# Denominators of a softmax from a running sum over four key tiles in place of two pair sums, with the tasks of a software pipeline moved to other slots

## The reference

```python
xt = jnp.transpose(x, (0, 2, 1))                 # 512 tokens, 256 channels
q = xt @ Wq.T
qh = q.reshape(B, T, 8, 32).transpose(0, 2, 1, 3)
scores = scale * jnp.einsum('bhqd,bhkd->bhqk', qh, qh)
logits = (scores * cmask + (1.0 - cmask) * NEG) * rmask
attn = jax.nn.softmax(logits, axis=-1)
ctx = jnp.einsum('bhqk,bhkd->bhqd', attn, qh)
out = ctx.reshape(...) @ Wo.T                    # and x = x + out, transposed back
```

## Time and profile before

| | |
|---|---|
| median of 3 runs | 2805.89 us (2802.98 to 2807.58) |
| profiled execution | 2816.45 us, its span 2814.6 us |
| TensorE matmul busy | 2633.3 us, 94% |
| VectorE busy | 2097.5 us, 75% |
| ScalarE busy | 1348.0 us, 48% |
| GpSimd busy | 914.2 us, 32% |
| mean granted TensorE clock | 0.984 |
| denominators' products (L706) | 480 passes, 605 ns each |
| adds on GpSimd (L407) | 120, 2349 ns each |

### The profile page before, as it was taken

How to read it: one execution, slowest core, us unless ns; L and a number is a source line. 1 busy time by engine, 2 the same in 40 slices (tenths; PEclk the granted TensorE clock), 3 DMA queues, 4 the chain that set the end, 5 groups by cost and what they waited for, 6 DMA issues and landing times. The chain is left out here.

```text
span 2814.6 us, 108219 instructions
## 1 busy us (share of the span) xinstructions
PE 2633.3 (94%) x46966; PEld 1503.7 (53%) x46966; DVE 2097.5 (75%) x4263; ACT 1348.0 (48%) x2344; POOL 914.2 (32%) x830
## 2 busy tenths in 40 slices
PE   8999999999989999999999999997999999999986
PEld 4333333333379898989999898983222222222221
DVE  5766666666788887888888887755777777777785
ACT  2555555555322222222322222211888787887876
POOL 1444444444022222222222222111244344344333
PEclk9999999999799999999999999998999999999999
DMA  2310111101100000000000000004344444544532
GB/s 66 94 55 28 54 37 46 55 28 43 27 14 0 0 0 0 0 0 0 0 0 0 0 0 0 0 5 108 74 107 116 107 106 112 114 104 112 115 91 52
DMA packets 120897, 132.05 MB, mean 47 GB/s; under 512 B 31800, under 2 KB 84944, under 8 KB 120674
## 3 DMA queue, kind: packets, MB, share of 16 engines
q1 hardware_dynamic: 114942, 123.12, 17.1%
q10 hardware_dynamic: 5760, 6.56, 0.8%
HBM read 85.29 MB, written 44.30 MB: 46 GB/s over the span
## 5 line engine op out<-in xcount | busy, mean ns | idle before, releaser
L912 PE MATMUL exp_ps<-region,gru_hT 128*16 128x128 f32 x16384 | 498.5, 274 | 39.3 <-DVE gru_hT L1039 7.8
L1582 DVE TENSOR_REDUCE x<-exp_ps 128x2 f32<-128x1024 f32 x352 | 426.0, 1221 | 104.8 <-PE exp_ps L1693 104.3
L912 PEld LDWEIGHTS exp_ps<-region,gru_hT 128*16 128x16 f32 x16384 | 428.3, 103 | 107.8 <-DVE gru_hT L1039 107.8
L845 POOL TENSOR_TENSOR xT<-xT,gru_hT 128x64 f32<-128x64 f32 x256 | 181.0, 707 | 824.6 <-DVE gru_hT L1039 815.6
L1508 ACT ACTIVATE region<-exp_ps,x 128x1024 f32<-128x1024 f32 x336 | 370.2, 1110 | 72.8 <-PE exp_ps L1664 72.8
L407 POOL TENSOR_TENSOR l_probs<-l_probs 128x1024 f32<-128x1024 f32 x120 | 281.1, 2349 | 297.7 <-ACT l_probs L483 220.1
L958 ACT ACTIVATE gru_r<-exp_ps 128x128 f32<-128x128 f32 x256 | 70.9, 277 | 588.1 <-PE exp_ps L912 588.1
L593 DVE TENSOR_REDUCE l_maxes<-exp_ps 128x2 f32<-128x1024 f32 x176 | 214.9, 1221 | 132.8 <-PE exp_ps L668 132.7
L997 DVE SCALAR_TENSOR_TENSOR xT<-x,condT,xT 128x512 f32<-128x512 f32 x420 | 311.0, 781 | 0.0
L897 PE MATMUL exp_ps<-region,gru_x_st 128*32 128x128 f32 x8192 | 272.1, 274 | 11.4 <-POOL gru_x_st L863 11.4
L1677 PE MATMUL bank<-region,x 128*17 128x512 f32 x2048 | 271.5, 602 | 6.7 <-ACT region L1508 3.6
(11 more groups left out here) (182 smaller groups left out, 4240.7 us busy)
## 6 DMA issues: line engine op xcount, KB each, us to landing
region<-key_query_scratch SPq DMA_DIRECT2D x128, 192.0 KB
key_query_scratch<-x SPq DMA_DIRECT2D x48, 256.0 KB, 2.5
key_query_scratch<-region SPq DMA_DIRECT2D x48, 256.0 KB, 2.5
region<-in_x SPq DMA_DIRECT2D x16, 512.0 KB, 4.8
l_xres<-in_x SPq DMA_DIRECT2D x16, 512.0 KB, 4.0
x_scratch<-x SPq DMA_DIRECT2D x16, 512.0 KB, 2.8
l_rden<-rden_scratch SPq DMA_DIRECT2D x120, 64.0 KB, 2.1
l_rden<-rden_scratch SPq DMA_DIRECT2D x240, 32.0 KB, 1.8
```

Of the source, the lines that this page charges most:

```text
L845: pool.tensor_tensor(dst, dst, hT[:, q, :, HALF:QW], ALU.add).then_inc(added, 1)
L912: last = pe.matmul(out[QW * j:QW * j + rows, cols], hT[:, p, k, state], group_of(wh[:, k, gate, :], j), start=False, stop=True, skip_group ...
L1582: dve.tensor_reduce(maxes[:, half, qt, head % HH:head % HH + 2], pairs[ring.place[2 * slot + 1]][:, :, :], AX_X, ALU.max).then_inc(taken[" ...
```

## The change

In every group of heads GpSimd adds the tile of each segment onto the next one, so that after three adds for each of two tiles the last tile holds the sum over all four key tiles: twelve adds a step in place of eight. TensorE then forms the denominators of a group with four products in place of eight, in slot 11 (first group) and in slot 3 of the next step (second group). The exponentials that overwrite a tile wait for the add that read it (`added`), or for the denominators in the case of the last tile. The denominators are taken out of PSUM in slots 12 and 4 (10 and 2 before), inverted in slot 7 (5), and multiplied in slots 11 and 13 (9 and 12). The maxima are shifted by four slots: tiles 0 to 11 of batch s + 1 in slots 4 to 15, tiles 12 to 15 in slots 0 to 3 of the next step; so `mtb` moves from slot 1 to 5, `mta` from 10 to 13, the splits from behind slots 7 and 15 to behind slots 11 and 3. `v1` moves from 5 to 6, `v0` from 13 to 14. SyncE loads x and mask in front of the denominators' transfers of the step. The last batch keeps its products over all tiles.

```diff
-    AT = {"mtb": 1, "q1": 3, "v1": 5, "mta": 10, "q0": 11, "v0": 13, "out": 15, "reciprocal": 5, "sums": 10}
-    SCALE = (9, 12)
+    AT = {"mtb": 5, "q1": 3, "v1": 6, "mta": 13, "q0": 11, "v0": 14, "out": 15, "reciprocal": 7, "sums": 10}
+
+    FIRST = 4
+    SCALE = (11, 13)
...
+        def tile_at(slot):
+
+            return (slot - FIRST) % SLOTS, 0 if slot < FIRST else 1
+
         order = []
         for slot in range(SLOTS):
-            order += [(slot, "st", slot, 0, 16), (slot, "max", slot, 1, 16)]
+            order += [(slot, "st", slot, 0, 16), (slot, "max", *tile_at(slot), 16)]
...
                 n = Counts(sp, s, PAIRS)
+                if active(s, 2) and not (isinstance(s, int) and s == -2):
+
+
+                    wait(sp, ready["q1"], n(1, 2))
+                    load_x(s + 2)
+                    wait(sp, kq_done[1], n(1, 2))
+                    load_mask(s + 2)
                 if active(s, -1):
 
                     store_den(1, n(2, 0))
...
-                if active(s, 2) and not (isinstance(s, int) and s == -2):
-
-
-                    wait(sp, ready["q1"], n(1, 2))
-                    load_x(s + 2)
-                    wait(sp, kq_done[1], n(1, 2))
-                    load_mask(s + 2)
...
+        def sums_made(s, seg, hp):
+
+            return 12 * s + 6 * (seg // 4) + 2 * (seg % 4 - 1) + hp + 1
...
-            def add_tiles(s, n, hp):
-
-                first, second = 2 * (2 * n % 4) + hp, 2 * ((2 * n + 1) % 4) + hp
-                wait(pool, taken["st"], 16 * s + 2 * (2 * n + 1) + hp + 1)
-                wait(pool, o_done, SEGS * s + 2 * n + 1)
-                pool.tensor_tensor(probs[:, first, :, :], probs[:, first, :, :], probs[:, second, :, :], ALU.add).then_inc(added, 1)
+            def add_tiles(s, seg, hp):
+
+                own, before = 2 * (seg % 4) + hp, 2 * (seg % 4 - 1) + hp
+                wait(pool, o_done, SEGS * s + seg + 1)
+                if seg % 4 > 1:
+                    wait(pool, added, sums_made(s, seg - 1, hp))
+                pool.tensor_tensor(probs[:, own, :, :], probs[:, own, :, :], probs[:, before, :, :], ALU.add).then_inc(added, 1)
 
             def step(s, par):
                 if active(s, 1):
                     set_masks(0, "mta", s + 1)
-                    set_masks(1, "mtb", s + 1)
-                if active(s, 0) and not (isinstance(s, int) and s == LAST):
-                    for n in range(SEGS // 2):
-                        for hp in range(2):
-                            add_tiles(s, n, hp)
+                for seg in range(SEGS):
+                    if seg == 3 and active(s, 1):
+
+                        set_masks(1, "mtb", s + 1)
+                    if active(s, 0) and s != LAST:
+                        for hp in range(2 if seg % 4 else 0):
+                            add_tiles(s, seg, hp)
...
-                        wait(act, d_done, SEGS // 2 * s + seg // 2 - 1)
+                        if s == LAST and seg >= 4:
+                            wait(act, d_done, 2 * s + seg // 2 - 1)
+                        elif seg % 4 == 3:
+                            wait(act, d_done, 2 * s + seg // 4)
+                        else:
+                            wait(act, added, sums_made(s if seg >= 4 else s - 1, (seg + 4) % 8 + 1, hp))
...
-            def denominators(s, n):
+            def denominators(s, grp):
+
+                wait(pe, added, sums_made(s, 4 * grp + 3, 1))
+                wait(pe, d_taken, 2 * s + grp)
+                for j in range(GH):
+                    last = pe.matmul(d_ps[QW * j:QW * j + QW, :], ones[:, :], probs[:, 6 + j // 2, j % 2, :], start=True, stop=True)
+                last.then_inc(d_done, 1)
...
-                    if slot % 4 == 1 and slot > 1 and active(s, 0):
-                        denominators(s, (slot - 5) // 4)
-                    if slot == 1 and active(s, -1):
-                        denominators(s - 1, SEGS // 2 - 1)
+                    if slot == 3 and active(s, -1) and s <= LAST:
+                        denominators(s - 1, 1)
+                    if slot == 11 and active(s, 0) and s != LAST:
+                        denominators(s, 0)
+                    if slot % 4 == 1 and slot > 1 and s == LAST:
+                        denominators_last((slot - 5) // 4)
+                    if slot == 1 and s == LAST + 1:
+                        denominators_last(3)
```

More of the change, by code:

```diff
@@ L301, in l0_part, with max_tile @@
         block = ctx.enter_context(nc.Block())
-        def max_tile(slot):
-            return slot // 8, slot % 8 // 2, 1 - slot % 2
+        def max_tile(tile):
+            return tile // 8, tile % 8 // 2, 1 - tile % 2
         @block.sync
@@ L469, in evac_den @@
             def evac_den(s, grp):
-                wait(act, d_done, SEGS // 2 * s + 2 * (grp + 1))
+                wait(act, d_done, 2 * s + grp + 1)
                 wait(act, den_stored, 16 * (2 * s + grp))
@@ L490, in step @@
                         evac_sums(s - 1, 1 - par, 1)
-                    if slot == 2 and active(s, -1) and not (isinstance(s, int) and s > LAST):
+                    if slot == 4 and active(s, -1) and s <= LAST:
                         evac_den(s - 1, 1)
@@ L502, in step @@
                         evac_sums(s, par, 0)
-                    if slot == AT["sums"] and active(s, 0) and not (isinstance(s, int) and s == LAST):
+                    if slot == 12 and active(s, 0) and s != LAST:
                         evac_den(s, 0)
@@ L572, in invert_last @@
             def invert_last(grp):
-                dve.wait_ge(d_done, SEGS // 2 * LAST + 2 * (grp + 1))
+                dve.wait_ge(d_done, 2 * LAST + 2 * (grp + 1))
                 dve.wait_ge(den_stored, 16 * 2 * LAST)
@@ L586, in step @@
                 for slot in range(SLOTS):
[L587 to L593, removed]
+                    tile, ahead = tile_at(slot)
+                    if active(s, ahead):
+                        half, qt, hp = max_tile(tile)
+                        wait(dve, ready["max"], 16 * (s + ahead) + tile + 1)
+                        if tile % 8 == 0:
+                            wait(dve, split_done, 2 * (s + ahead - 1) + half + 1)
+                        dve.tensor_reduce(maxes[:, half, qt, 2 * hp:2 * hp + 2], tasks.bank_of("max", tile)[:, :, :], AX_X, ALU.max)\
                            .then_inc(taken["max"], 1)
-                        if slot % 8 == 7:
-                            split(half, "mtb" if half else "mta", s + 1)
+                        if tile % 8 == 7:
+                            split(half, "mtb" if half else "mta", s + ahead)
                     for kind, idx, off in (("q1", 1, 1), ("q0", 0, 2)):
@@ L607, in step @@
                         invert_last(s - LAST)
-                    if isinstance(s, int) and (s, slot) in ((LAST, 13), (LAST + 1, 2)):
+                    if isinstance(s, int) and (s, slot) in ((LAST, 14), (LAST + 1, 2)):
                         scale_last(s - LAST)
@@ L650, in products @@
                 grp, kt = seg // 4, seg % 4
-                half, qt, mp = max_tile(slot)
-                at = {kind: next(n for n, t in enumerate(tasks.tasks) if t[1] == kind and t[2] == slot) for kind in ("st", "max")}
+                tile, ahead = tile_at(slot)
+                half, qt, mp = max_tile(tile)
+                at = {kind: next(n for n, t in enumerate(tasks.tasks) if t[0] == slot and t[1] == kind) for kind in ("st", "max")}
                 if active(s, 0):
@@ L661, in products @@
                                   max_rows[row:row + NPART, grp, :], start=True, stop=False)
-                if active(s, 1):
-                    if slot % 8 == 0:
-                        wait(pe, kq_done[half], s + 2)
+                if active(s, ahead):
+                    if tile % 8 == 0:
+                        wait(pe, kq_done[half], s + ahead + 1)
                     tasks.free(pe, s, at["max"])
+                    of = (par + ahead) % 2
                     for i in range(2):
                         rows = slice(QW * (2 * mp + i), QW * (2 * mp + i) + QW)
-                        last = pe.matmul(tasks.bank(at["max"])[:, i, :], kq[rows, 1 - par, half, qt * P:qt * P + P],
-                                         kq[rows, 1 - par, half, :], start=True, stop=True)
+                        last = pe.matmul(tasks.bank(at["max"])[:, i, :], kq[rows, of, half, qt * P:qt * P + P],
+                                         kq[rows, of, half, :], start=True, stop=True)
                     last.then_inc(ready["max"], 1)
@@ L689, in weighted_sums, with denominators_last @@
                 last.then_inc(o_done, 1)
-            def denominators(s, n):
+            def denominators(s, grp):
[4 more added lines that the diff above has]
+                last.then_inc(d_done, 1)
+            def denominators_last(n):
                 grp = n // 2
                 if n % 2 == 0:
[L695 to L704, removed]
+                    pe.wait_ge(d_taken, 2 * LAST + grp)
```

(6 more changed lines are left out.)

## The result

| | before | after |
|---|---|---|
| median | 2805.65 us (2802.98 to 2807.58) | 2840.34 us (2837.08 to 2846.35) |
| ratio | | 1.0127, 95% interval 1.0108 to 1.0146 |
| profiled execution, its span | 2816.45, 2814.6 | 2846.35, 2844.6 |
| step of the first layer | 43.72 us | 46.61 us |
| adds on GpSimd, denominators' passes | 120, 480 | 180, 240 |

What follows compares the result with a forecast made beforehand. The self-attention was taken as bound by a ring through the exponential, about 2.4 us a slot, or longer TensorE work. 13 x (2.3 + 1.3) + 1.3 + 2.9 + 0.7 - 4.6 = +47 gave 2853 us, range 2826 to 2864.

Steps and rivals of the forecast that it cites:

- The ring: First-layer slots: maxima wait for the previous slot's exponential; a slot costs about 2.4 us or its TensorE work, if longer.
- empty slots: Slots with the products and nothing else (7 before; 1, 7, 9 after): claimed to stay near 2.4 us.
- The groups that are kept: Denominators' groups in slots 3 and 11, behind q1 and q0: claimed +1.00 us each, 2.99 to 3.99.
- The second scaling: Slot 13: claimed to stand still in a GpSimd add and delay slot 15's maxima, +1.3 us a step.
- rival 2: The ring holds but the scaling waits at no cost: +2.3 us a step alone, 2834.5 us; chance 0.27.
- The step as a whole: Steady first-layer step: claimed 2.3 + 1.3 us longer, about 47 us long.
- the ring's part: Sum of slot changes from moving denominators, v1, v0 and transpositions, without the scaling: claimed +2.3 us a step.
- Prologue: Slots 0 to 3 before the steps lose their maxima; 9.3 us become 4.7: claimed -4.6 us.
- step 15: Last step gets four slots of maxima: claimed between 0 and 4 x 0.6 us, taken as 0.7.
- GpSimd's adds: Eight adds a step become twelve, 18.7 to 28.0 us: claimed 0 for new waits on ScalarE and TensorE.
- The loads: x and mask loads issued earlier on SyncE: claimed 0, at worst 1.
- Rival 3: TensorE's clock falls to 1.2 GHz in slots 7 to 10 of steady steps: +64 us, 2917; chance 0.06.

Runs made afterwards that it cites:

- the kernels with both repairs: Changed kernel with denominators' groups in slots 5 and 13 and scalings in slots 10 and 11: 2820.45 us; its three variants 2819.88, 2823.14 and 2811.03 us.

## Why the prediction was right, and where it was off

- **The ring sets plain slots, not TensorE.** Shown: empty slots 2.37 to 2.43 us, 4 us of extra work for 0.28.
- **The groups that are kept cost 1.00 us each behind q1 and q0.** Shown by moving them: 1.95 us a step.
- **The second scaling stands in an add.** Shown: request and length (2.81) as forecast; priced at 1.3 us a step, it measured 1.07. Counted from slot 12's start, slot 15 began at +8.75 with the stall, and at +7.57 in the run without it, where I had +9.05 and +7.75; and slot 15 itself is 0.10 longer without it. By the median alone rival 2 (2834.5 us, the scaling at no cost) lies nearer to 2840.34 than the forecast of 2853 does. It is the length of the scaling in the trace, and the run that moves it, that decide for the forecast's mechanism.
- **The step as a whole** was mis-sized: +3.6 forecast, +2.89 measured. Beside the scaling, the ring's part was +2.3 and measured 2.90 - 1.07 = +1.8. I took 2.47 us for an empty slot from the one slot 7 of before; in the new order slots 1 and 9 take 2.37 (slot 1 falls by 0.08) and slot 7 takes 2.43. Slot 13 shed 0.35, not 0.15 (v0 with a group had taken 2.80, not v1's 2.66), and slots 5 and 6 came out 0.06 lower each than I had them. Over 13 steps the difference of 0.7 us makes 9 of the 12 us by which the forecast was too high.
- **Prologue** (-4.6) **and step 15** (+0.7): not seen singly, since the clock blurs both in the two profiled executions, by some 7 to 9 us. The run with extra work in the empty slots, whose prologue ran at the upper clock, has the first `out` 2.5 us earlier than before (134.99 us against 137.45), with step 1 in it, which is 3.2 us longer there (2.9, and 0.28 for the extra work). That makes an estimate of -5.6 for the prologue and step 0, where I had -4.6 + 1.3 = -3.3. Step 15 took 45.75 us at a granted clock of 1.00 after the change; no trace of the kernel before has it at that clock.
- **GpSimd's adds hold up neither ScalarE nor TensorE.** The trace agrees: no such wait between 190 and 700 us.
- **The loads cost or bring nothing**: for their new place true; I had not seen that in the old place they would have cost 0.6 us a step.
- **Rival 3, the clock in steady steps**, did not come in the changed kernel. In variants of it the clock fell in single steady steps, mostly behind an idle time of 2.8 us that a late scaling had made, but in two traces also without one.

The sum of what was measured: 12 steps +34.4, step 14 +2.3, prologue with steps 0 and 1 about -2.7 where the clock held: +34.0, and the medians differ by 34.7. That they agree to 0.7 us is luck, since step 15 is not in this sum and the unchanged rest of the kernel varies by 9 us from trace to trace.

## What to carry to other kernels

Before work is taken off an engine that a profile calls 97% busy, compare two slots that differ by just that work; if they last equally long, its removal pays nothing, and what counts is whether the work that stays moves into a slot where the engine is the bound. Where VectorE and GpSimd run side by side, place operations with two SBUF inputs by the times of GpSimd's adds, and with slack for the transfer in front of them; of those with one input, the cast of 0.20 us was held up too, the reciprocal was not. A schedule should be judged by the distribution of its steps: the kernels with both repairs had shorter typical steps and a worse median than the kernel that they were to beat.

## What the runs showed of the hardware

- A VectorE operation with two SBUF inputs that asks 0.05 us behind the start of a GpSimd add ends some 0.55 us after that add has ended (2.81 us for 0.68). So it was in 11 of the 14 steps of the changed kernel, at 2.79 to 2.81 us; in the other three the transfer came later and it took 1.40 to 2.51. The reciprocal of one SBUF input keeps its 0.34 us inside adds, and so do the reductions out of PSUM with 1.22; the cast of one SBUF input does not (2.37 us in an add before, 0.20 outside one after).
- Twelve idle times of TensorE of 2.8 to 2.9 us stand in the steady steps of five traces; around eleven of them the granted clock fell to 0.50, mostly for some 3 us. Slots with idle times of 1.0 to 1.1 us keep it at 1.00 in all steady steps of the changed kernel, but in step 10 of two variants it fell to 0.50 behind such slots.
- Row-packed products of two kinds (two float32 products each, into different row blocks) take 1.07 us when they run side by side, and 1.02 and 1.06 us one after the other when one kind has to wait for an exponential.
